# Loads held back and reordered, kernel 1 split, last turning split, streams of quad 1 reordered in a two-layer convolution

## The reference: what is computed

```python
x = x + _L0_conv_ref(_gn(x), L0_conv_weight, L0_conv_bias)   # 9x9, 32 to 32 channels, zero padding
x = x + _L1_conv_ref(_gn(x), L1_conv_weight)                 # 5x5, 32 to 32 channels, reflect padding
```

## Time and profile before

| | |
|---|---|
| median of 3 runs | 240.6 us (240.59 to 241.17) |
| the profiled execution | 241.09 us, its span 239.3 us |
| busy: PE (TensorE), DVE (VectorE), ACT (ScalarE), POOL | 232.4, 211.6, 157.8, 4.5 us |
| TensorE's granted clock | full, all through |
| chain that ended last, by engine | PE 57%, DVE 26%, ACT 8%, issue 5%, DMA 3% |
| moved by DMA | 17.24 MB; HBM read 5.57 MB, written 4.72 MB |

### The profile page before, as it was taken

How to read it: one execution, slowest core, us unless ns; L and a number is a source line. 1 busy time by engine, 2 the same in 40 slices (tenths; PEclk the granted TensorE clock), 3 DMA queues, 4 the chain that set the end, 5 groups by cost and what they waited for, 6 DMA issues and landing times.

```text
span 239.3 us, 4173 instructions
## 1 busy us (share of the span) xinstructions
PE 232.4 (97%) x1451; PEld 144.9 (61%) x1451; DVE 211.6 (88%) x460; ACT 157.8 (66%) x329; POOL 4.5 (2%) x12
## 2 busy tenths in 40 slices
PE   7999999999799999999999999999999999999995
PEld 7755656556466665556666665556666665555554
DVE  5989999898999999999989999999997459978943
ACT  6879899889489577999637694537459003569310
POOL 1000000230000000000000000000000000000000
PEclk9999999999999999999999999999999999999999
DMA  6980122320034000003422000162020002521123
GB/s 207 370 354 5 25 64 55 75 48 3 0 92 123 3 1 0 3 0 101 131 85 94 5 4 0 29 175 112 1 101 0 0 0 57 157 102 57 47 99 99
DMA packets 8709, 17.24 MB, mean 72 GB/s; under 512 B 3312, under 2 KB 5616, under 8 KB 8688
## 3 DMA queue, kind: packets, MB, share of 16 engines
q1 hardware_dynamic: 7712, 16.64, 21.1%
q10 hardware_dynamic: 976, 0.34, 0.6%
HBM read 5.57 MB, written 4.72 MB: 43 GB/s over the span
## 4 chain that ended last, share of the span: by engine, by line
PE 57%; DVE 26%; ACT 8%; issue 5%; DMA 3%; SPq 0%; DVEq 0%; ACTq 0%
PE banks L1508 29%; PE banks L1491 28%; DVE X L805 5%; DVE lo L772 3%; DMA X<-in_x 3%; ACT junk L1108 3%; DVE whl L565 2%; DVE wl L590 1%; ACT P L1141 1%; ACT hi L1164 1%; DVE work L560 1%; ACT arg L1188 1%; DVE arg L548 1%; ACT work L1206 1%; DVE X L812 1%
## 5 line engine op out<-in xcount | busy, mean ns | idle before, releaser
L1491 PE MATMUL banks<-hi,whl 128*128 128x360 f16 (+4 forms) x576 | 98.0, 318 | 2.2 <-ACT hi L1164 1.5
L1491 PEld LDWEIGHTS banks<-hi,whl 128*128 128x128 f16 x576 | 55.5, 98 | 36.7 <-issue 1.9
L1491 PE MATMUL banks<-lo,whl 128*128 128x376 f16 (+4 forms) x288 | 51.2, 318 | 0.0
L1108 ACT ACTIVATE junk<-X 128x576 bf16<-128x576 f32 x56 | 41.2, 737 | 2.8 <-DMA X<-in_x 0.8
L1491 PEld LDWEIGHTS banks<-lo,whl 128*128 128x128 f16 x288 | 27.9, 97 | 16.6
L1508 PE MATMUL banks<-hi,wh 128*128 128x384 f16 (+1 forms) x165 | 31.5, 320 | 0.2 <-ACT hi L1164 0.2
L1508 PE MATMUL banks<-lo,wh 128*128 128x384 f16 (+1 forms) x165 | 31.5, 320 | 0.0
L1508 PE MATMUL banks<-hi,wl 128*128 128x384 f16 (+1 forms) x165 | 31.5, 320 | 0.0
L1164 ACT CAST hi<-work 128x416 f16<-128x416 f32 x32 | 16.6, 536 | 16.9 <-PE banks L1508 11.9
L1154 ACT ACTIVATE work<-work,gof,gsc 128x26 f32<-128x26 f32 (+1 forms) x48 | 24.9, 609 | 3.6 <-DVE gof L666 3.6
L1164 ACT CAST hi<-s 128x384 f16<-128x384 f32 x32 | 15.4, 508 | 17.2 <-DVE s L739 10.9
(11 more groups left out here) (137 smaller groups left out, 233.4 us busy)
## 6 DMA issues: line engine op xcount, KB each, us to landing
X<-in_x SPq DMA_DIRECT2D x8, 576.0 KB, 10.1
out<-X SPq DMA_DIRECT2D x7, 576.0 KB, 2.8
work<-X SPq DMA_DIRECT2D x8, 432.0 KB, 3.8
whl<-work SPq DMA_DIRECT2D x24, 64.0 KB, 2.0
work<-X SPq DMA_DIRECT2D x8, 144.0 KB, 3.6
stage<-in_w SPq DMA_DIRECT2D x1, 640.0 KB, 8.0
work<-X SPq DMA_DIRECT2D x32, 12.0 KB, 2.3
out<-X SPq DMA_DIRECT2D x1, 384.0 KB, 2.6
```

The source lines that it names most:

```text
L1108: nc.scalar.activation(waste, image(n, m), function, accum_out=sums[c][:, col:col + 1]).then_inc(sums_done[c], 1)
L1491: ins = nc.tensor.matmul(dst[:, :, y0:y1], w[1][:, i, t * P:(t + 1) * P], src[:, :, y0 + IMG * dx:y1 + IMG * dx], start=(first and part == ...
```

## The change

- SP waits, after issuing pairs 0 and 1, until pair 0 has landed; then it issues pairs 2 to 7, then the bias (before on ScalarE's queue), then layer 2's weights (before behind pair 1).
- VectorE scales kernel 1 in two operations (384 and 256 columns) and ScalarE casts it in two. `casts` counts one more from kernel 1 on: kernel 1 needs 2, kernel 2 needs 4. TensorE begins stream 1 with one cast less. The second wait, before tap 1, now holds for streams 1 and 2.
- The last turning (kernel 6 to kernel 4) is done by eight DMAs: four for the high half with a semaphore, four for the low half with another. TensorE waits for the low one only before the third part.
- VectorE makes the outer streams of quad 1 ahead of `rows1(0, 1)`, whose two groups of three updates stand before and behind the two low halves.

```diff
 def casts(i):
     at = FIRST_ORDER.index(i)
-    return at + 1 + (1 if at >= FIRST_ORDER.index(2) else 0)
+    return at + 1 + sum(at >= FIRST_ORDER.index(j) for j in SPLIT)
...
             load(1)
-            sp.dma_start(stage[:, :, :], w1).then_inc(stage_loaded, 16)
+            sp.wait_ge(x_loaded[0], 16)
             for n in range(2, NP):
                 load(n)
-            for at, i in enumerate(FIRST_ORDER):
+            sp.dma_start(bias_c[1][:, :], bias).then_inc(bias_loaded, 16)
+            sp.dma_start(stage[:, :, :], w1).then_inc(stage_loaded, 16)
+            def turn_half(at, i, half, landed):
+
+                sp.wait_ge(turning, 2 * (at - len(TURN_BANKS)) + half + 1)
+                for k in range(RB):
+                    sp.dma_start(whl[(RB - 1 - k) * C:(RB - k) * C, half, MIRROR[i], NT * P:],
+                                 turn_at[k * C:(k + 1) * C, at % TURNS, half, :]).then_inc(landed, 16)
+
+            for at, i in enumerate(FIRST_ORDER[:-1]):
                 if i not in TURN_BANKS:
                     turn(at, i)
+            turn_half(7, FIRST_ORDER[-1], 0, turned[LAST_TURNED])
+            turn_half(7, FIRST_ORDER[-1], 1, last_low_turned)
...
-                flat1 = slot(1).rearrange("p k (r o) -> p (k r) o", o=C)
-                done(stt(flat1, flat1, W_SCALE, krec[:, :].unsqueeze(1).to_broadcast([P, NT * RB, C]), ALU.mult, ALU.mult))
-                MARK["weights", 1] = count[0]
+                for half, taps in enumerate(STEPS2):
+                    at = slice(*taps)
+                    flat1 = slot(1)[:, at, :].rearrange("p k (r o) -> p (k r) o", o=C)
+                    done(stt(flat1, flat1, W_SCALE, krec[:, :].unsqueeze(1).to_broadcast([P, (taps[1] - taps[0]) * RB, C]), ALU.mult, ALU.mult))
+                    MARK["weights", 1, half] = count[0]
...
                 far1(1)
-                rows1(0, 1)
                 streams1_ends(1)
+                rows1(0, 1, (0,))
                 low_halves(1, 1, range(2, 4))
+                rows1(0, 1, (1,))
                 middle1(0, 2)
...
-            act.dma_start(bias_c[1][:, :], bias).then_inc(bias_loaded, 16)
...
             high_half(1, 0, 0)
-            high_kernel(1)
+            high_kernel_parts(1)
             normalise1(0, range(2))
             high_half(1, 0, 1)
-            high_kernel_two()
+            high_kernel_parts(2)
...
-                        pe.wait_ge(wh1_done, casts(i) - (1 if i == 2 else 0))
+                        pe.wait_ge(wh1_done, casts(i) - (1 if i in SPLIT else 0))
...
                         pe.wait_ge(turned[i], 16 * RB)
+                    if qd == 0 and not first and part == 2 and i == LAST_TURNED:
+                        pe.wait_ge(last_low_turned, 16 * RB)
                     for t in taps:
-                        if qd == 0 and first and part == 0 and i == 2 and t == STEPS2[1][1] - 1:
+                        if qd == 0 and first and part == 0 and i in SPLIT and t == STEPS2[1][1] - 1:
                             pe.wait_ge(wh1_done, casts(2))
```

More of the change, by code:

```diff
@@ L73 @@
 FIRST_ORDER = (1, 2, 0, 7, 3, 4, 5, 6)
+SPLIT = (1, 2)
 MIRROR = {1: 1, 2: 2, 0: 7, 7: 0, 3: 5, 5: 3, 4: 6, 6: 4}
@@ L79 @@
                (0, "turned"), (4, "made"), (5, "made"), (5, "turned"), (6, "made"), (6, "turned"), (3, "turned"), (4, "turned"))
+LAST_TURNED = MIRROR[FIRST_ORDER[-1]]
 X_SCALE = 64.0
@@ L264, in build @@
         turned = {i: sem(f"turned{i}") for i in range(8)}
+        last_low_turned = sem("last_low_turned")
         hi_done = {c: sem(f"hi{c}_done") for c in (1, 2)}
@@ L796, in middle1, with rows1 @@
                 stt(pd[1][:, :], product1(qd, k), -f, mb[1][:, :], ALU.mult, ALU.add).then_inc(mid_done[1], 1)
-            def rows1(qd, g):
-                for which, src, factors in ((0, ps, EVEN_ROWS), (1, pd, ODD_ROWS)):
+            def rows1(qd, g, halves=(0, 1)):
+                for which in halves:
+                    src, factors = ((ps, EVEN_ROWS), (pd, ODD_ROWS))[which]
                     dve.wait_ge(mid_done[1], 6 * qd + 2 * g + which + 1)
@@ L1192, in high_kernel, with high_kernel_parts @@
                 nc.scalar.copy(made_taps(wh, i), weight1(i)).then_inc(wh1_done, 1)
-            def high_kernel_two():
+            def high_kernel_parts(i):
                 for step, taps in enumerate(STEPS2):
                     at = slice(*taps)
-                    act.wait_ge(dve_w, MARK["weights", 2, step])
-                    nc.scalar.copy(made_taps(wh, 2)[:, at, :], slot(2)[:, at, :]).then_inc(wh1_done, 1)
+                    act.wait_ge(dve_w, MARK["weights", i, step])
+                    nc.scalar.copy(made_taps(wh, i)[:, at, :], slot(i)[:, at, :]).then_inc(wh1_done, 1)
             def turn_kernel(i, part):
```

## The result

The changed kernel takes 242.65 us (median of 4 runs, 242.59 to 242.73) against 240.76 for the kernel before in the same comparison (240.59 to 241.17): a ratio of 1.0077, 95% interval 1.0061 to 1.0093. It is slower by 1.9 us; 1.2 were forecast (241.8, range 241.0 to 242.9). The sign, the path of the delay and the range held. The size was 0.85 us off; more than half of that is the step by which the sum was carried from one execution to the median, and the range held the result only because it had been drawn wide enough for the second rival (242.5), whose number is nearer than the forecast.

What follows compares the result with a forecast made beforehand. Bound: a chain of waits through VectorE and ScalarE until about 100 us, then TensorE's matmuls. Head -0.7, halves -0.1, wait +2.2, outer streams -0.2 make +1.2 on 241.09, 242.3; less 0.5 to the median, 241.8 us (range 241.0 to 242.9).

Steps and rivals of the forecast that it cites:

- the second rival: Start of the kernel: the reordered loads do not bring pair 1 earlier; total +1.9, 242.5 us; chance 0.13.
- The new wait: TensorE before tap 1 of stream 1: idle 2.3 us until kernel 2's second cast, delaying stream 0's cast; +2.2 us.
- nothing absorbs it: Up to 50 us no idle time takes up the delay; rival of partial absorption: about 241.0 us, chance 0.14.
- The head: Start of the kernel: reordered loads land pair 1 earlier, so ScalarE and VectorE run earlier; -0.7 us.
- the step to the median: From the profiled execution's 241.09 plus 1.2, 242.3, down 0.5 because the runs' median, 240.6, is lower: 241.8 us.
- Kernel 1 in halves: VectorE's scale and ScalarE's cast of kernel 1 in two: ScalarE gains 0.1 us, which TensorE cannot use.
- The last turning: Eight DMAs for four: TensorE's wait of about 0.5 us only moves eight matmuls back; gain 0.
- Outer streams first: Quad 1, near 60 us: TensorE's idle time at 63.9 moves to the fifth stream; VectorE loses 0.2 idle; -0.2 us.
- The rival that ends faster: The new wait at tap 1 of stream 1 is covered and costs nothing: -0.9, 239.7 us; chance 0.09.
- The clock: TensorE's clock falls to 1.2 GHz in the stall; 27 matmuls take 4.2 us more: 246 us; chance 0.03.

Runs made afterwards that it cites:

- experiment 10: The kernel before, unchanged, profiled once more for the landing of pair 1: 240.57 us (8 runs).
- experiment 1: The changed kernel with TensorE's wait before tap 1 asking for casts(i), so stream 1 waits only for kernel 1's own casts: 240.63 us, ratio 1.0002.
- experiment 2: The kernel before with only the wait before tap 1 extended to stream 1, asking for kernel 2's second cast: 242.84 us, ratio 1.0095.
- experiment 8: The changed kernel with ScalarE's copy of turned kernel 2's high half behind the cast of stream 0: 242.31 us, ratio 1.0080.
- experiment 3: The kernel before with the change's loads alone (SP waits for pair 0; bias and layer 2's weights last): 240.54 us, ratio 0.9995.
- experiment 5: The kernel of experiment 1 with the last turning in four DMAs again: 240.64 us, ratio 0.9999.
- experiment 4: The kernel before with the change's order of streams of quad 1 alone: 240.74 us, ratio 1.0002.

## Why the prediction was right, and by how much it was off

- **The new wait** (+2.2) was the right step and carries the result. The stall itself was 1.9 and not 2.3, because TensorE came to it at 18.10 and not at 17.7; the release, which alone moves what follows, was where the sum had it. Against the kernel before as it usually runs (experiment 10), the cast of stream 0 moves from 24.18 to 26.21, 2.0 us; experiments 1 and 2 give 2.0 and 2.3 in whole times. The way was the one written down, TensorE to ScalarE's copy to the cast to VectorE, with the turning at 25.26 for 25.2. That nothing absorbs it was right too, and for one more reason than I gave: experiment 8 shows a second way, over TensorE's sums.
- **The head** (-0.7) and the step to the median (-0.5) do not go together, and this is where the forecast went wrong. Against the execution of 241.09 the head's term is right: ScalarE takes up pair 1 at 7.29 for 8.16, its cast of stream 2 comes 0.72 earlier (19.35 for 20.07), and TensorE is released at 20.56 for 20.5. But that execution had pair 1 0.8 late, and the kernel as it usually runs has not, as far as experiment 10's one profiled execution, at 240.60, shows; the loads are worth 0.04 us there (experiment 3). By taking off the 0.5 by which the execution was above the median I counted its lateness twice, once as a gain of the change and once as the distance to the median. Either sum alone is near: 241.09 + 1.2 is 242.3, and with the head at nothing and no such step it is the second rival's 242.5. Of the 0.85 between 241.8 and 242.65, 0.5 is this step, 0.2 the outer streams (below) and 0.14 the cast of stream 0, at 26.21 for 26.07.
- **Why pair 1 lands when it does** stays open. No execution with the new order of loads waits for pair 1, but two of the four with the old order do not either, and SP's wait, the bias and layer 2's weights were only ever moved together. I read 242 GB/s beside the bias as the Trainium skill's rule of turns at work ("DMA: Bandwidth & Descriptors", on queues, rings and completion order). The low rate is no sign of that: in the same microsecond the kernel before moved 303 GB/s in experiment 10 with the bias in flight, and the changed kernel, with the bias not yet issued, moves 148 and does not wait for pair 1:

```profile
6.00:7.00 1.00, 1.00 (x6) 1.00 (x5) 0.96 (x3) 0.90 (x4) 0.00 (x0) 1.00 0.82 148
```

The rule itself is neither shown nor refuted by a run here.
- **Kernel 1 in halves** (-0.1): ScalarE's idle 0.16 went, and its cast of stream 2 came at 19.35; against 19.60 in experiment 10 that is 0.25, of which 0.14 is pair 0, taken up at 5.44 instead of 5.58. TensorE, at 18.1, could not use it, as said.
- **The last turning** (0): as worked out, SP's eight issues and TensorE's wait of 0.4 before the third part; experiment 5 confirms that it is worth nothing either way.
- **Outer streams first** (-0.2): TensorE's idle time moved as told, to 72 and 74 us (experiment 4 and the changed kernel). The 0.2 for VectorE did not come. VectorE lost its wait of 0.2 for ScalarE's cast and got another as long: in the changed kernel the combination behind the last of the row updates starts 1.63 us after the first of three, where the three before them take 1.41. That this is a wait for their last write is my reading of the code's semaphores, not shown by a run.
- **The rival that ends faster** fell: the stall of 1.9 was there, ScalarE's copy waited 1.07 for the turning, and experiment 2 prices the wait at 2.3. **The clock** did fall in a stall, in one run of experiment 2 (and by the mean clock in one of experiment 8), but not in the changed kernel, and for less than its price: 1.7 us where I had 4.2, since it was back at 2.4 GHz before the 27 matmuls were through.

## What to carry to other kernels

A wait that names another item's count does not show in a count of bytes and operations; here one such number cost 2 us. Follow what stands behind the waiting instruction, and behind the engine that waits for that. Before a stall is priced from a profile, profile the same kernel twice; a late load in one execution may be that execution's and not the kernel's, and a sum against that execution must not also be corrected to the median when the same lateness makes the distance. When a gate is opened, look for the next one downstream (72, 78, 166 us here) before judging the edit by its time.

## What the runs showed of the hardware

- In one execution of experiment 2's kernel 2.6 us of idle time after three matmuls, behind a dense stretch, was followed by about 3.4 us at 1.2 GHz, which cost 1.7 us. Its mean granted clock is 0.993; the other four runs have 1.0 and no such loss. Stalls of 1.9 and 2.2 us in the profiled executions of the changed kernel and of experiment 8 left the clock at 2.4 GHz. One run of experiment 8 took 243.66 where the others took 242.19 to 242.31, and its mean clock is 0.993 as well; there is no trace of it, so where the clock fell is not shown.
- SP takes 0.63 us to issue a DMA of the turnings, whether it moves 64 KB (2.50 for four) or 32 KB (5.02 for eight).
- With an unchanged kernel and order of loads the wait for pair 1 varied from 0 to 0.8 us between executions, and the two profiled executions of it at the ends of that, 241.09 and 240.60, differ by 0.49, their casts of stream 0 by 0.46. With the new order the wait was 0 in eight executions, and the one for pair 0 varied from 0 to 0.7. What makes a landing late was not tried.
